# A fused attention and ternary feed-forward kernel on one core: part of its preparation in another order, one pass on GpSimd

## The reference, cut to what matters

```python
# x: 4 sequences x 1024 tokens x 512; all float32
xn = layernorm(x)
c_Q  = rms_norm(xn @ Wq_down, q_norm_w)               # 192
q_nop, q_pe = c_Q @ Wq_up, c_Q @ Wq_pe                # 16 heads x (128 + 64)
c_KV = rms_norm(xn @ Wkv_down, kv_norm_w)             # 128
k_nop, v = split(c_KV @ Wkv_up)                       # 8 heads, each for 2 query heads
k_pe = rms_norm(xn @ Wk_pe, k_pe_norm_w)              # 64, shared by all heads
q_pe, k_pe = rotary(q_pe), rotary(k_pe)
attn = softmax(causal(q @ k.T * 192 ** -0.5))
y = (attn @ v) @ Wo
x_q = where(xn > 0.33, 0.5, where(xn < -0.33, -0.5, 0))
w_q = where(weight > 0.2, 0.6, where(weight < -0.2, -0.6, 0))
out = x + y + x_q @ (w_q + rram_variation).T
```

## Time and profile before

| | |
|---|---|
| median of 3 runs | 1722.79 us (1718.19 to 1723.05) |
| profiled execution, its own time | 1720.58 us |
| its span | 1718.8 us |
| TensorE busy over the span | 1665.9 us, 97% |
| VectorE, ScalarE, GpSimd busy | 77%, 66%, 34% |
| mean granted TensorE clock | 0.991 |

### The profile page before, as it was taken

One profiled execution on the slowest core, in us unless ns is written; L12 is line 12 of the kernel. 1 busy time (PEld: TensorE's weight loads), 2 busy tenths in 40 slices (PEclk: granted clock), 3 DMA queues, 4 the chain that ended last, 5 costly groups with the idle time before them and its releaser, 6 DMA issues.

```text
span 1718.8 us, 30082 instructions
## 1 busy us (share of the span) xinstructions
PE 1665.9 (97%) x9579; PEld 845.3 (49%) x9579; DVE 1328.5 (77%) x3370; ACT 1129.4 (66%) x2464; POOL 583.6 (34%) x1046
## 2 busy tenths in 40 slices
PE   4789999999999999999999999999999999999999
PEld 3445455544544445545454445555454444554444
DVE  6687888778788787777878788877877878777765
ACT  6676766657667666666767566666766766666663
POOL 2223333333334233333333333333333323343320
PEclk9799999999999999999999999999999999999999
DMA  9347888978978888986878978886897988997886
GB/s 280 72 80 144 151 147 147 151 133 151 163 134 152 146 153 153 165 153 114 161 134 162 175 137 151 149 151 127 154 159 143 162 139 146 160 159 141 143 154 128
DMA packets 910775, 254.57 MB, mean 148 GB/s; under 512 B 897368, under 2 KB 899930, under 8 KB 910298
## 3 DMA queue, kind: packets, MB, share of 16 engines
q1 hardware_dynamic: 899920, 228.99, 76.7%
q10 hardware_dynamic: 9162, 17.37, 3.5%
q0 software_dynamic: 1536, 6.29, 1.1%
HBM read 19.79 MB, written 8.39 MB: 16 GB/s over the span
## 4 chain that ended last, share of the span: by engine, by line
PE 81%; DVE 5%; issue 5%; DMA 3%; ACT 3%; POOL 2%; SPq 1%; ACTq 0%; DVEq 0%; POOLq 0%
PE bank L647 6%; PE bank L648 6%; PE bank L649 6%; PE bank L650 6%; PE bank L752 5%; PE bank L754 5%; PE bank L753 5%; PE bank L691 4%; PE bank L693 4%; PE bank L692 4%; PE bank L659 4%; DMA XT<-XS 2%; DVE F L1464 2%; PE bank L420 2%; PE bank L421 2%
## 5 line engine op out<-in xcount | busy, mean ns | idle before, releaser
L1040 ACT ACTIVATE P<-P,nm 128x512 f32<-128x512 f32 (+7 forms) x512 | 394.4, 771 | 449.7 <-DVE nm L1450 449.5
L1450 DVE CUSTOM_DVE_ANT_0 P<-bank,mask,neg 128x512 f32<-128x512 f32 (+7 forms) x512 | 399.1, 815 | 270.6 <-PE bank L659 259.2
L1681 POOL TENSOR_SCALAR sn<-sm 128x1 f32<-128x1 f32 x512 | 203.8, 399 | 934.1 <-ACT P L1040 923.6
L1035 ACT ACTIVATE F<-P,rc 128x512 f16<-128x512 f32 (+7 forms) x512 | 378.6, 767 | 81.2 <-DVE rc L1458 60.0
L1464 DVE SCALAR_TENSOR_TENSOR F<-P,rc,F 128x512 f16<-128x512 f32 (+7 forms) x512 | 416.0, 825 | 2.7 <-ACT F L1035 2.3
L647 PE MATMUL bank<-K,Q 128*128 128x512 f16 (+3 forms) x760 | 248.7, 327 | 0.0
L648 PE MATMUL bank<-K,Q 128*128 128x512 f16 (+3 forms) x760 | 248.7, 327 | 0.0
L649 PE MATMUL bank<-K,Q 128*128 128x512 f16 (+3 forms) x760 | 248.7, 327 | 0.0
L650 PE MATMUL bank<-K,Q 128*128 128x512 f16 (+3 forms) x760 | 248.6, 327 | 0.0
L752 PE MATMUL bank<-WO,YH 128*128 128x512 f16 x512 | 194.3, 379 | 3.4 <-DVE YL L1470 2.0
L754 PE MATMUL bank<-WO,YL 128*128 128x512 f16 x512 | 194.1, 379 | 0.0
(11 more groups left out here) (230 smaller groups left out, 2878.7 us busy)
## 6 DMA issues: line engine op xcount, KB each, us to landing
out<-X ACTq DMA_DIRECT2D x31, 256.0 KB, 3.8
X<-in_x ACTq DMA_DIRECT2D x28, 256.0 KB, 3.1
FT<-F SPq DMA_TRANSPOSE x348, 4.3
wo<-in_Wo POOLq DMA_DIRECT2D x4, 1024.0 KB, 7.7
V<-CC SPq DMA_DIRECT2D x32, 64.0 KB, 2.8
Q<-QS SPq DMA_TRANSPOSE x128, 4.0
X<-in_x SPq DMA_DIRECT2D x4, 256.0 KB, 7.3
kv<-in_Wkv_up POOLq DMA_DIRECT2D x1, 1024.0 KB, 11.6
```

Of the source, the lines that this page charges most:

```text
L1035: return e.eng.activation(dst, src, ACT.Copy, scale=scale)
L1040: e.eng.activation(m.P[:, u % 4, 0:w], m.P[:, u % 4, 0:w], ACT.Exp, bias=m.nm[:, u % 8:u % 8 + 1], scale=-1.0, accum_out=m.sm[:, u % 8:u % ...
L1450: e.eng.tensor_tensor_reduce(out=m.P[:, u % 4, 0:w], in0=m.pS[u % 2][:, off:off + w], in1=m.mask[:, 1024 - w:1024], scale=m.neg[:, :], sca ...
```

## The change

Nothing is computed otherwise; operations change their place in their queues, and one changes its engine.

- TensorE: the first down product goes behind the second head group's query turns and the sums of the query scale, and ahead of its key turn. The feed-forward scale's sum goes ahead of the second down product. `ffn(0)` goes ahead of `up(3)`, and the sums of the output weights' squares go behind `up(3)` and into another bank.
- ScalarE: `turned(1)` goes ahead of the first tile's down copy and norms; the square of the feed-forward weights ahead of the second rotation; the high copies of the feed-forward weights ahead of the second tile's parts and of the last two output squares; the third tile's down copy and norms from round 6 to behind the rounds.
- VectorE: the first ternary pass leaves its queue; the other two come earlier; the feed-forward scale and the low parts of the weights go ahead of other work; the third tile's signs go into round 0 and its `rms` behind the first half head group of the loop.
- GpSimd: it does the first ternary pass, behind the keys of the first tile, then waits for the landing of V before it issues the last two loads of the output weights.

```diff
--- before.py
+++ after.py
@@ -559,14 +559,13 @@
     e.wait_ge(s.ld_ident, 16)
     turn_queries(0)
     turn_keys(0)
-    e.wait_ge(s.ld_ua, 16)
-    tiles.down(0, m.pY[0])
     turn_queries(1)
-    turn_keys(1)
     e.wait_ge(s.q_sq, 3)
     e.wait_ge(s.b_sq, 2)
     e.wait_ge(s.scale, 1)
     sums(3, 8)
+    tiles.down(0, m.pY[0])
+    turn_keys(1)
     products(0)
     turn_queries(2)
     turn_keys(2)
@@ -579,21 +578,21 @@
     queries.up_pe(1)
     queries.up(1)
     products(3)
+    e.wait_ge(s.f_sq, 1)
+    sums(2, 3, m.pY[1])
     tiles.down(1, m.pY[0])
     queries.up_pe(2)
     queries.up(2)
-    e.wait_ge(s.f_sq, 1)
-    sums(2, 3, m.pY[1])
     for c in range(4):
         turn_f(c)
     queries.up_pe(3)
+    e.wait_ge(s.scale, 2)
+    tiles.ffn(0, m.pY[1])
     queries.up(3)
     e.wait_ge(s.o_sq, 4)
+    e.wait_ge(s.ropeq, NG)
+    sums(8, 12)
     e.wait_ge(s.cr, 2)
-    sums(8, 12, m.pY[0])
-    e.wait_ge(s.scale, 2)
-    tiles.ffn(0, m.pY[1])
-    e.wait_ge(s.sco, 1)
     tiles.ffn(1, m.pY[0])
 
 
@@ -988,10 +987,10 @@
     turned(0)
     e.wait_ge(s.ld_pa, 16)
     square(m.pa[:, :, :], 6, (s.q_sq, 3), scale=m.wq[:, 0:1])
+    turned(1)
     tiles.down_out(0, m.pY[0])
     tiles.squares(0)
     tiles.rms_root(0)
-    turned(1)
     tiles.ln_root(1)
     tiles.parts_hi(0)
     products_out(0)
@@ -1006,27 +1005,26 @@
     queries.queries_hi(0)
     products_out(2)
     output_squares(1, 2)
+    e.wait_ge(s.tern, 3)
+    square(m.fr[:, :, :], 2, (s.f_sq, 1), junk=m.JB)
     queries.rotated_hi(1)
     queries.queries_hi(1)
     products_out(3)
-    e.wait_ge(s.tern, 3)
-    square(m.fr[:, :, :], 2, (s.f_sq, 1), junk=m.JB)
     tiles.down_out(1, m.pY[0])
     tiles.squares(1)
     tiles.rms_root(1)
-    output_squares(2, 3)
-    tiles.parts_hi(1)
-    queries.rotated_hi(2)
-    queries.queries_hi(2)
-    output_squares(3, 4)
-    tiles.ln_root(2)
     e.wait_ge(s.scale, 2)
     for c in range(4):
         e.wait_ge(s.ft, c + 1)
         copy(m.wfh[:, c, :], fold_bank(m, "f", c), m.fsc[:, :]).then_inc(s.wfh, 1)
+    tiles.parts_hi(1)
+    queries.rotated_hi(2)
+    queries.queries_hi(2)
+    tiles.ln_root(2)
+    output_squares(2, 4)
+    tiles.norm(2)
     queries.rotated_hi(3)
     queries.queries_hi(3)
-    tiles.norm(2)
     tiles.x_hi(2)
 
 
@@ -1095,11 +1093,10 @@
             scaled_hi(u - 1)
         outputs_out(2 * u)
         outputs_out(2 * u + 1)
-        if u == 6:
-            tiles.down_out(2, m.pO)
-            tiles.squares(2)
-            tiles.rms_root(2)
     scaled_hi(4 * AHEAD - 1)
+    tiles.down_out(2, m.pO)
+    tiles.squares(2)
+    tiles.rms_root(2)
     for n in range(N):
         t, g = divmod(n, NG)
         for p in range(2):
@@ -1296,9 +1293,7 @@
     def feed_forward(x):
 
         e.wait_ge(s.ld_ffn, 32)
-        if x == 0:
-            e.eng.tensor_scalar(m.tern[:, :, :], m.fw[:, :, :], -0.2, None, ALU.is_lt).then_inc(s.tern, 1)
-        elif x == 1:
+        if x == 1:
             e.wait_ge(s.tern, 1)
             e.eng.scalar_tensor_tensor(out=m.fw[:, :, :], in0=m.fw[:, :, :], scalar=0.2, in1=m.tern[:, :, :],
                                        op0=ALU.is_gt, op1=ALU.subtract).then_inc(s.tern, 1)
@@ -1396,44 +1391,41 @@
     turned(2)
     tiles.x_signs(1)
     products_lo(1)
-    feed_forward(0)
+    feed_forward(1)
     queries.rotate(0)
     turned(3)
     queries.queries_lo(0)
-    feed_forward(1)
+    feed_forward(2)
     queries.rotate(1)
     products_lo(2)
     queries.queries_lo(1)
-    feed_forward(2)
     products_lo(3)
-    tiles.rms(1)
-    tiles.stats(2)
-    queries.rotate(2)
     e.wait_ge(s.norms, 3)
     half(m.G[:, 2:3], m.pY[1][:, 2:3])
     powers(slice(2, 3), m.G[:, 2:3])
     e.eng.tensor_scalar(m.fsc[:, :], m.AL[:, 2:3], -0.5, None, ALU.mult).then_inc(s.scale, 1)
-    e.wait_ge(s.scale, 2)
-    queries.queries_lo(2)
-    tiles.parts_lo(1)
-    queries.rotate(3)
+    tiles.rms(1)
+    tiles.stats(2)
+    queries.rotate(2)
     for c in range(4):
         e.wait_ge(s.wfh, c + 1)
         e.eng.scalar_tensor_tensor(out=m.wfl[:, c, :], in0=fold_bank(m, "f", c), scalar=m.fsc[:, :], in1=m.wfh[:, c, :],
                                    op0=ALU.mult, op1=ALU.subtract).then_inc(s.wfl, 1)
+    queries.queries_lo(2)
+    tiles.parts_lo(1)
+    queries.rotate(3)
+    tiles.ln(2)
+    tiles.ffn_out(0, m.pY[1])
     e.wait_ge(s.norms, 4)
-    link(e.eng.tensor_reduce(m.B[:, 4:5], m.pY[0][:, 8:12], AX_X, ALU.max))
+    link(e.eng.tensor_reduce(m.B[:, 4:5], m.pO[:, 8:12], AX_X, ALU.max))
     settle()
     half(m.G[:, 11:12], m.B[:, 4:5])
     link(e.eng.tensor_tensor(m.G[:, 14:15], m.G[:, 9:10], m.G[:, 11:12], ALU.mult))
     settle()
     powers(slice(4, 5), m.G[:, 14:15])
     e.eng.tensor_scalar(m.invo[:, :], m.IV[:, 4:5], 2.0 ** -11, None, ALU.mult).then_inc(s.sco, 1)
+    tiles.ffn_out(1, m.pY[0])
     queries.queries_lo(3)
-    tiles.ln(2)
-    tiles.ffn_out(0, m.pY[1])
-    tiles.ffn_out(1, m.pY[0])
-    tiles.x_signs(2)
 
 
 def vector_attention(e, m, s, tiles, queries):
@@ -1514,10 +1506,10 @@
         if u:
             outputs_lo(2 * u - 2)
             outputs_lo(2 * u - 1)
+        if u == 0:
+            tiles.x_signs(2)
         if u == 3:
             tiles.stats(3)
-        if u == 7:
-            tiles.rms(2)
     inverse(4 * AHEAD - 1)
     outputs_lo(14)
     outputs_lo(15)
@@ -1564,7 +1556,7 @@
                 if p and joined(n):
                     values_lo(n)
                 scaled_lo(u + 1)
-            if t and t + LEAD - 1 < T and (g, p) == (0, 0):
+            if t + LEAD - 1 < T and (g, p) == (0, 0):
                 tiles.rms(t + LEAD - 1)
             if t + LEAD - 1 < T and (g, p) == (0, 1):
                 tiles.parts_lo(t + LEAD - 1)
@@ -1658,6 +1650,8 @@
     outputs.load(1)
     tiles.rotate_keys(0)
     tiles.keys(0)
+    e.eng.tensor_scalar(m.tern[:, :, :], m.fw[:, :, :], -0.2, None, ALU.is_lt).then_inc(s.tern, 1)
+    e.wait_ge(s.v_in, 16)
     outputs.load(2)
     outputs.load(3)
     tiles.x_lo(1)
```

## The result

| | before | after |
|---|---|---|
| median of 5 runs each | 1719.87 us (1718.19 to 1723.05) | 1712.10 us (1710.95 to 1713.89) |
| profiled execution, its own time | 1720.58 us | 1713.89 us |
| its span; mean granted clock | 1718.8 us; 0.991 | 1712.1 us; 0.994 |

The ratio is 0.9947, with a 95% interval of 0.9931 to 0.9963: 9.1 us faster (6.4 to 11.9). The same kernel was timed again, beside three of the experiments (`after_again`): 1710.05 us against 1718.60, ratio 0.9946 (0.9934 to 0.9959).

What follows compares the result with a forecast made beforehand. TensorE is busy almost throughout from 135 us, so only idle time in the front can be won: 7.5 + 1.9 = 9.4 us, giving 1711.2 for the profiled execution, 1713.4 against the median; range 1708 to 1720.

Steps and rivals of the forecast that it cites:

- Sums before the down product: Front: query-scale sums by about 23.4 us, ScalarE's CC at 29.7 instead of 32.19, 2.5 us earlier.
- GpSimd's queue: Front: first tile's key parts end at about 35.8 instead of 36.11, gaining only 0.3 us; GpSimd and VectorE exclude each other.
- The ternary pass: On GpSimd, 2.2 us (35.8 to 38.0), estimates 2.0 to 4.6, far end 9.3; VectorE's following pass ends at 39.3.
- rival A: GpSimd becomes the bound: pass costs 4.6 us or locks fall badly, L484 2.4 later; gain 7.0, 1715.8 us; chance 0.20.
- Late loads: Front: two output loads held back, C lands at about 40, V at 41, L484 starts at 42.5, gain 4.4 us.
- Feed-forward weights: Front: second and third ternary passes, scale and low parts sooner; ffn(0) at 64.5 to 64.9 instead of 74.38, 9.5 to 9.9.
- Given back: up(3) and output sums now follow ffn(0); L611 at 73.0 to 74.6 instead of 81.60, gain 7.0 to 8.6, taken 7.5.
- Norms behind the rounds: Third tile's ScalarE norms leave the rounds: gain 1.9 us, bounds 0 and 3.5 (clock stays high, ffn(2) takes 1.8).
- Rival B: Gain mostly absorbed: second tile's transpose collides with late loads, lands 56.6; 1718 to 1720 us; chance 0.16 with the last rival.
- Rival C: Slower: V lands at 47.2, GpSimd stands waiting, L611 at 83.2, 1724.4 us; decided by V at about 46; chance 0.09.
- the last rival: C still waits because the first two loads alone fill the engines; late-loads gain gone, 1718 us; chance 0.16 with Rival B.

Runs made afterwards that it cites:

- e8: Changed kernel with GpSimd's ternary pass ahead of the first two output loads, by a semaphore of its own: 1712.16 us, ratio 0.9958.
- e2: Changed kernel with the first ternary pass back on VectorE, right ahead of the second, GpSimd's wait for V kept: 1709.57 us, ratio 0.9939.
- e5: Changed kernel with the first ternary pass back on VectorE and GpSimd's wait for V taken away: 1712.89 us, ratio 0.9960.
- e10: Changed kernel, ternary pass in VectorE's early gap, third tile's low part behind output scale, second's ahead of V wait and late loads: 1710.78 us, ratio 0.9941.
- e1: Changed kernel without GpSimd's wait for V, the ternary pass still on GpSimd: 1711.93 us, ratio 0.9952.
- e9: Changed kernel with GpSimd's low part of the third tile made to wait for the output scale: 1709.87 us, ratio 0.9940.

## Why the prediction was right, point by point

The forecast was 9.4 us of gain; the ratio says 9.1. Most landmarks agree, but two steps were wrong in opposite directions, so part of the agreement is luck, and a third cost came on top. Two signs of the prediction did not come as written: the new pass took over 5 us (5.40 by itself, 6.46 in the changed kernel), which it had named as a sign of being wrong, and C took 6.3 us and not under 5.

1. **Sums before the down product.** Sums 22.71 (forecast 23.4), CC 30.04 (29.7). Right in what the order gives at CC: 3.0 us there against the experiment with the down product first, 2.2 against the kernel before, 2.5 in the forecast.
2. **GpSimd's queue.** Wrong. The key parts ended at 33.96, 2.15 us earlier than before, not 0.3. I let VectorE's `pa` pass fall on top of them; it came at 33.85, behind them, and the loads' issue started at 29.94, not 30.71. That VectorE and GpSimd shut each other out did hold (3.54, 5.36 and 0.98 us above). The sentence of the Trainium skill ("SBUF — State Buffer", section "Who interferes with whom") on two-input instructions fits the 0.98 us. The 5.36 us were a single-input `tensor_scalar` with a scalar operand: the same section counts that operation among those that can take the shared ports in a 2-port mode, which the forecast had not used. With two inputs the `pbw` pass was let go 1.9 us before GpSimd's ended (39.73 - 1.28 = 38.45, against 40.39), which "fully blocks" doesn't cover. In `e8` the operation behind the held one is recorded from 31.36, 1.8 us before GpSimd's pass ended, so there too something was let go ahead of that end.
3. **The ternary pass.** The term that was most mis-sized: 2.2 us forecast from the memset, 5.40 measured, above my 4.6 and below the far end of 9.3. One input was not cheaper: the pass takes 2.6 ns per element, the two-input pass of the earlier trace rows 2.3. Steps 2 and 3 cancel, by luck: the `pbw` pass was forecast to end at 39.3 and ended at 39.73. So rival A's cause was there (the pass over 4.6 us), and its effect, 2.4 us on L484, was nearly what the pass cost (2.3 against `e2`); it did not show against the forecast since the queue was 1.8 us earlier than I had thought.
4. **Late loads.** C at 40.3 (about 40), V at 41.2 (41), L484 at 42.67 (42.5), XT issued at 46.06 (45.9) and landed at 51.7 (50 to 52). Right in the landmarks, and the largest of the parts that have a run of their own: 6 us at L484, 3.3 us of the time (`e2` against `e5`). C's landing agrees although it was issued at 34.04 and the forecast had the key parts at 35.8: it went by the loads and not by its own issue, as the table above shows, and the forecast had put it behind the end of the loads (about 38) too. What I put down to the wait for V is done by the pass ahead of it, which keeps the loads back until 40.0 alone; with the pass on VectorE the wait is needed.
5. **Feed-forward weights.** `fr` ready at 50.53 (50.7), its square at 53.50 (53.8, though the forecast's own terms add up to 53.6), the scale at 58.75 (59.5), low parts at 64.93 (64.4 to 64.9), `ffn(0)` at 65.07 (64.5 to 64.9). The landmarks are right; how much of the time this step brings was not tested by itself (some 3 us with step 6, by the estimate under `e5`).
6. **Given back.** L610 at 74.66 (73.0 to 74.6): 6.9 us of gain, 7.5 taken. `ffn(0)`, `up(3)` ran at the low level (0.63 us for an L421) until 70.5, `ffn(1)` at the high one (0.38), which should have given 73; but L610 waited 1.60 us for the scale chain and `ffn_out`. The 0.75 of `ffn_out` were in the forecast; the other 0.8, GpSimd's low part of the third tile in the way of the chain, were not.
7. **Norms behind the rounds.** L420's wait fell from 2.66 to 0.60 us; the stretch from L610 is 2.06 us shorter (1.9). ScalarE's chain, now at 93.87 to 96.32, delays nothing before L420. Right. The upper bound's condition was met as well: `ffn(2)` ran at the higher clock level, 0.38 us for an L421, against this row of the kernel before:

```profile
104.71 0.64 PE L421 MATMUL bank<-wfl,XT 128*128 128x512 f16 x1
```

Behind `ffn(2)` the gain was 10.4 us (next score product at 96.39 against 106.84). It didn't last: TensorE then waited 1.61 us for the query parts and ran at the lower level from 101.6 on, and at the next score products (104.77 against 112.79) the gain was 8.0.

Rival B's mechanism is real (XT 11.0 us in `e10`), but not in the changed kernel: the two loads went out at 41.49, XT landed 10.2 us behind them at 51.7, and it was wanted at 53.9. B let it land 10.7 us behind its own issue, and the 4.6 us between the loads and XT are why it took only 5.6 of its own. Rival C needed V after 46; it came at 41.2. C did not stay late, so the last rival fell too.

Against the profiled execution the sum was 2.7 us too good (1711.2 against 1713.89). At the first store the gain was 9.9; then 3.2 went in the loop, which the forecast had held unchanged. The cause of the late FT and XT transposes there stays open; the profile of `after_again` gains 0.8 us over the same stretch, so I read it as scatter between executions. The median came out 1.3 us below the forecast one (1712.10 against 1713.4), since the forecast stood on the three runs of before that it had (median 1722.79, five runs give 1719.87).

## What to carry to other kernels

Where a small transfer on the critical path runs beside loads of a megabyte, look at how many stand ahead of it and when they were issued: here it landed 10 to 11 us behind the issue of two and 16 behind that of the first of four, whenever it was issued itself. An idle engine is not a free place for a pass if it and the busy one hold each other up, as VectorE and GpSimd did here: look at what the busy engine does in these microseconds, and price the pass from a row of the same kind, not from a memset. And let a landmark that is met count as evidence for a step only when the steps before it are met too.

## What was not expected of the hardware

- A VectorE operation of 128x2 elements took 5.36 us, as long as GpSimd's 128x2048 pass beside it, while the `pbw` pass, larger and with two inputs, was released some 1.9 us before the GpSimd pass ended (an estimate: its end, less the 1.28 us that it takes alone).
- GpSimd's single-input compare from float32 to float16 took 5.40 us for 2048 elements per partition; the same on VectorE takes 1.21 to 1.23.
- The same DMA transpose of C took 3.7 us when two loads of 1 MB had been issued 6.6 us before it, 5.3 to 6.7 when it was 3.8 to 5.3 us, and 10.7 and 11.8 with four ahead; with two it landed 10.1 to 10.6 us behind their issue each time.
- In two executions L484 ran at the lower clock level (0.42 us, `e1`) and at the higher one (0.27 us, the changed kernel) after starting within a microsecond of each other. `e9` had L484 at the lower level and its second down product at the higher, the changed kernel the other way round, and in `e9` `ffn(0)` came 1.1 us sooner, counted from the sums: one order of work does not fix the clock of its stretches.
